# A fused state-space layer and feed-forward block: the last half-operand of each group sum moves from TensorE to VectorE, and the gate moves one scan later

## The reference, cut to what matters

```python
proj = layernorm(x) @ in_proj_w               # 1024 -> 2 x 2048
xc, z = split(proj)                           # channel-major, 2048 channels
xc = silu(conv_b + causal_conv4(xc))
dt, Bm, Cm = rmsnorm of (xc @ x_proj_w)       # 64, 16, 16 columns
dt = softplus(dt @ dt_proj_w + dt_bias)
h[n] = exp(dt * A[n]) * h[n] + dt * Bm[n] * xc   # 16 states per channel, along the rows
ys = sum over n of h[n] * Cm[n]
y  = (ys + D * xc) * silu(z)
x  = x + y @ out_proj_w
x  = x + layernorm(x) @ dequantised(W).T + bias
```

## Time and profile before

| what | us |
| --- | --- |
| median of 3 runs | 4703.04 |
| lowest and highest | 4701.97, 4705.40 |
| the profiled execution | 4697.21 |
| its span in the trace | 4695.4 |
| mean granted TensorE clock | 0.972 of full speed |

### The profile page before, as it was taken

How to read it: one execution, slowest core, us unless ns; L and a number is a source line. 1 busy time by engine, 2 the same in 40 slices (tenths; PEclk the granted TensorE clock), 3 DMA queues, 4 the chain that set the end, 5 groups by cost and what they waited for, 6 DMA issues and landing times.

```text
span 4695.4 us, 80181 instructions
## 1 busy us (share of the span) xinstructions
PE 4448.9 (95%) x26656; PEld 4049.0 (86%) x26656; DVE 4160.0 (89%) x5745; ACT 3542.4 (75%) x8848; POOL 4039.2 (86%) x2942
## 2 busy tenths in 40 slices
PE   7788989999999999999999999999999999999889
PEld 6567879989898998989989898998989889898779
DVE  3898989989899998989989899998989989899981
ACT  3777787877778787777877878787787777778760
POOL 0898989989898998989989898998989899899990
PEclk9889999999999999999999999999999999999999
DMA  7324243353434435343353534334353443434232
GB/s 255 130 79 161 99 159 139 114 186 133 173 129 161 145 138 175 124 178 128 123 188 123 177 137 165 137 128 173 138 180 120 145 165 129 165 127 155 90 115 94
DMA packets 160285, 678.56 MB, mean 145 GB/s; under 512 B 21120, under 2 KB 30080, under 8 KB 110720
## 3 DMA queue, kind: packets, MB, share of 16 engines
q1 hardware_dynamic: 141440, 639.88, 39.0%
q10 hardware_dynamic: 18432, 33.56, 1.9%
HBM read 618.32 MB, written 55.05 MB: 143 GB/s over the span
## 4 chain that ended last, share of the span: by engine, by line
PE 59%; DVE 20%; POOL 7%; issue 6%; ACT 5%; DMA 1%; SPq 0%; DVEq 0%; POOLq 0%; ACTq 0%
PE g L767 13%; PE gx L594 13%; PE ys L574 12%; DVE hb L1342 11%; PE ys L614 9%; PE g L689 4%; POOL dbx L486 4%; DVE hc L1290 4%; DVE gx L1238 2%; POOL half L494 2%; PE ys L604 2%; DVE bst L1218 2%; PE gx L581 2%; ACT hb L1061 1%; PE hb L853 1%
## 5 line engine op out<-in xcount | busy, mean ns | idle before, releaser
L1342 DVE TENSOR_TENSOR_SCAN hb<-hb,dbx 128x512 f32<-128x512 f32 x2048 | 2498.0, 1220 | 108.0 <-ACT hb L1061 84.4
L486 POOL TENSOR_TENSOR dbx<-dtx,bb 128x1024 f32<-128x1024 f32 x1024 | 2421.0, 2364 | 60.1 <-DVE hb L1342 34.9
L1061 ACT ACTIVATE hb<-dt,a_neg 128x256 f32<-128x256 f32 x4096 | 1789.5, 468 | 66.3
L494 POOL TENSOR_TENSOR half<-hc 128x512 f32<-128x512 f32 x1024 | 1303.1, 1273 | 135.4 <-DVE hc L1290 120.4
L1290 DVE TENSOR_TENSOR hc<-hb,cb 128x512 f32<-128x512 f32 x2048 | 1378.9, 673 | 0.0
L574 PE MATMUL ys<-half,ident 128*128 128x256 f32 x4096 | 1073.2, 389 | 133.4 <-POOL half L494 119.2
L574 PEld LDWEIGHTS ys<-half,ident 128*128 128x128 f32 x4096 | 757.2, 194 | 254.3 <-POOL half L494 151.3
L767 PEld LDWEIGHTS g<-wo,ybuf 128*128 128x128 f32 x7680 | 954.0, 198 | 20.2 <-issue 1.3
L767 PE MATMUL g<-wo,ybuf 128*128 128x128 f32 x7680 | 966.7, 281 | 0.6 <-issue 0.6
L614 PE MATMUL ys<-xnT,wz 128*128 128x256 f32 x4096 | 928.8, 380 | 1.6 <-DVE ybuf L1301 1.6
L594 PE MATMUL gx<-xnT,wx 128*128 128x256 f32 x3968 | 904.5, 381 | 4.3 <-DMA wx<-in_win 2.6
(11 more groups left out here) (105 smaller groups left out, 2766.1 us busy)
## 6 DMA issues: line engine op xcount, KB each, us to landing
wz<-in_win SPq DMA_DIRECT2D x128, 1024.0 KB, 4.8
wx<-in_win SPq DMA_DIRECT2D x124, 1024.0 KB, 4.8
wo<-in_wout SPq DMA_DIRECT2D x123, 1024.0 KB, 4.9
wf<-wf_scratch SPq DMA_DIRECT2D x113, 512.0 KB, 3.2
xc_scratch<-xcn ACTq DMA_DIRECT2D x128, 256.0 KB, 2.1
xcs<-xc_scratch SPq DMA_DIRECT2D x128, 256.0 KB, 5.0
bb<-bc_scratch SPq DMA_DIRECT2D x64, 512.0 KB, 7.5
cb<-bc_scratch SPq DMA_DIRECT2D x64, 512.0 KB, 6.7
```

The lines of the kernel that those rows point to most:

```text
L486: nc.gpsimd.tensor_tensor(dbx[:, k % 2, :].rearrange("p (n t) -> p n t", n=NQ), dtx[:, S % 2, a, :].unsqueeze(1).to_broadcast([P, NQ, T]), ...
L494: nc.gpsimd.tensor_tensor(half[:, k % 4, :], hc[:, k % 2, 0:HALF], hc[:, k % 2, HALF:GW], ALU.add).then_inc(halves, 1)
L1061: ins = nc.scalar.activation(h[:, m * T:(m + 1) * T], dt[:, j % 2, a, :], ACT.Exp, scale=a_neg[:, ds((2 * j + a) * N + 2 * v + m, 1)])
L1342: nc.vector.tensor_tensor_scan(h[:], h[:], dbx[:, k % 2, w * UW:(w + 1) * UW], 0.0, ALU.mult, ALU.add).then_inc(scans, 1)
```

## The change

The last group of each half (groups 3 and 7) gets one product on TensorE instead of two. The other operand is added by VectorE onto the PSUM bank (`last_sum`), at the place where the gate stood, and the gate itself comes one scan later. GpSimd waits, before it overwrites the fourth of the four `half` buffers, for the gate that follows the `last_sum` that read it.

```diff
             def group_sum(S, k):
                 pool.wait_ge(hcs, after(UNITS * S + 2 * k + 2))
                 pool.wait_ge(sum_mm, after(8 * S + k - 3))
+                if k % NQ == NQ - 1:
+
+                    pool.wait_ge(y_ready, after(2 * S + k // NQ))
...
                 a, q = divmod(k, NQ)
                 pe.wait_ge(halves, after(8 * SG + k + 1))
-                for i in range(2):
+
+                for i in range(1 if q == NQ - 1 else 2):
                     mm = nc.tensor.matmul(ys[a][:, 0:T], ident[:], half[:, k % 4, i * T:(i + 1) * T],
-                                          start=False, stop=(q == NQ - 1 and i == 1), skip_group_check=True)
+                                          start=False, stop=(q == NQ - 1), skip_group_check=True)
                 mm.then_inc(sum_mm, 1)
...
+            def last_sum(SP, a):
+
+                k = NQ * (a + 1) - 1
+                dve.wait_ge(sum_mm, after(8 * SP + k + 1))
+                dve.wait_ge(halves, after(8 * SP + k + 1))
+                nc.vector.tensor_tensor(ys[a][:, 0:T], ys[a][:, 0:T], half[:, k % 4, T:HALF], ALU.add
+                                        ).then_inc(summed, 1)
+
             def y_gate(SP, a):
 
                 chunk, jp = divmod(SP, PAIRS)
-                dve.wait_ge(sum_mm, after(8 * SP + NQ * (a + 1)))
+                dve.wait_ge(summed, after(2 * SP + a + 1))
...
                     product(1)
+                    late_sum()
+                    scan(3)
                     late_y()
-                    scan(3)
                     product(2)
...
                     product(9)
+                    last_sum(S, 0)
+                    scan(11)
                     y_gate(S, 0)
-                    scan(11)
                     product(10)
...
+            last_sum(LAST - 1, 1)
             y_gate(LAST - 1, 1)
```

More of the change, by code:

```diff
@@ L212, in build_program @@
         a_exp = sem("a_exp")
-        conv, scans, hcs, y_ready = sem("conv"), sem("scans"), sem("hcs"), sem("y_ready")
+        conv, scans, hcs, y_ready, summed = (sem("conv"), sem("scans"), sem("hcs"), sem("y_ready"),
+                                             sem("summed"))
         xp_add, o_add, f_add = sem("xp_add"), sem("o_add"), sem("f_add")
@@ L1352, in late_product, with late_sum @@
                             times_c(S - 1, UNITS - 1)
+                    def late_sum():
+                        if was.scan and not (first and c == 0):
+                            last_sum(S - 1, 1)
                     def late_y():
```

## The result

| us | before | changed |
| --- | --- | --- |
| median | 4702.5 | 4796.8 |
| lowest and highest | 4701.7, 4705.4 | 4792.2, 4797.9 |
| ratio, 95% interval | | 1.0197 (1.018 to 1.0215) |
| profiled execution: span | 4695.4 | 4790.3 |

A forecast was written before the change was run, and what follows sets the result against it. TensorE was taken to set the ordinary interval of 33.20 us. Terms of 79 + 7 - 2 + 6 + 1.5 = + 92 us on 4697.2 gave 4789, with the median 5.8 above it 4795 us; range 4772 to 4838.

The forecast's parts named there:

- The loop: Group 3 on TensorE, VectorE's gates, `x_proj`, back to group 3: 34.17 us against 33.20, 0.97 us longer per ordinary step.
- The price of `last_sum`: Each addition on VectorE, two per step, was taken to cost 0.39 us, with bounds 0.33 and 0.40.
- The stall ahead of `x_proj`: In ordinary steps TensorE idles some 1.6 us for the late gate; VectorE idles some 1.8 us ahead of `last_sum`.
- The other intervals: Those of 34.4, 36.4 and 43.1 us, at each chunk's end, change by + 0.61, + 1.17 and - 0.04 us.
- The clock in the last step: Rival: TensorE's clock falls behind two stalls of about 1.5 us, 12 x 1.75 = + 21 us: 4816; chance 0.25.
- The sum over the chunks: Chunks 2 to 13 add 79 us, chunk 14 7, chunk 1 - 2, chunk 0 6, chunk 15 1.5: + 92 us.
- What was priced at nothing: GpSimd's new waits for gates, and `z_in_proj(1)` on TensorE waiting for the gate of half 0, cost nothing.
- Rival 2: The gate's new place at `x_proj` costs nothing and TensorE's relief counts: - 0.8 us in 67 intervals, 4657 us; chance 0.05.

The follow-up runs named there:

- e5: The kernel before with the late gate alone moved behind scan 3 and no sum moved: 4759.4 us, ratio 1.0131.
- e6: The changed kernel with `x_proj` behind `out_proj(1)` in ordinary steps and behind `out_proj(0)` in steps j = 0 and 7: 4683.3 us, ratio 0.9966.
- e2: The kernel before with both gates moved, behind scan 3 and scan 11, and no sum on VectorE: 4719.0 us, ratio 1.0043.
- e4: The changed kernel with `x_proj` behind `out_proj(1)` on TensorE in ordinary steps, steps j = 0 and 7 as they are: 4701.0 us, ratio 1.0003.
- e1: The changed kernel with both gates back ahead of the scans, right behind the sums on VectorE: 4729.2 us, ratio 1.0066.

## Why the prediction was right, point by point

The forecast was 4795 us and the measurement 4796.8. The mechanism is the one that was forecast; that the number came within 2 us is luck. In chunks 2 to 13 the price of `last_sum` and the intervals that hold it came out 13 us lower, and a fall of the clock that the forecast left to a rival took 13 us more; the two cancel.

- **The loop.** Right, with every part found: in the changed kernel the loop is 0.63 + 18.87 + 0.40 + 0.06 + 14.07 = 34.03 us, and the 0.13 that it is short of the forecast is the price of the two sums. e5 gives the late gate's move (33.20 to 33.81: + 0.61), and the sums give the rest, - 0.43 + 0.34 + 0.33 = + 0.24, against a measured 34.04 - 33.81 = + 0.23. Of + 0.84 us per ordinary step three quarters come from a gate that was moved and one quarter from sums that were added. The prediction had 0.97.
- **The price of `last_sum`** was the mis-sized term: 0.33 to 0.34 us from its start to the next, not 0.39, and a duration of 0.42 us. I had taken it from the convolution, for the write to PSUM that the two have in common; the gate, which has the operation in common, would have been right. The formula of the Trainium skill, "VectorE: DVE Perf Modes", section on the TRN2 errata, gave an estimate of 424 ns, and the trace agrees: the sum's mean on the page of the profile is 424:

```profile
L1304 DVE TENSOR_TENSOR ys<-ys,half 128x256 f32<-128x256 f32 x256 | 108.6, 424 | 243.5 <-PE ys L579 243.0
```

- **The stall ahead of `x_proj`**: 1.6 us predicted, 1.39 measured, and VectorE's wait at the sum 1.8 against 1.88.
- **The other intervals**: + 0.61, + 1.17 and - 0.04 were forecast; + 0.40, + 0.95 and + 0.2 were measured where the clock holds in the last step. Where it falls, the last is - 0.7 (42.3 us against 43.3).
- **The clock in the last step** was a rival with 0.25, and it happened, in every other chunk and for 3.1 us instead of 1.75. In six of twelve chunks that is + 18 us, of which the interval behind gives some 5 back: 13 us, where the forecast had nothing and the rival, in all twelve chunks, 21. I had priced it from a single stall in chunk 1; here the slow stretch was longer. From start to start `x_proj` lost 0.84 us (1.81 against 0.97), and the 16 products of `out_proj(0)` alone 1.67 us of duration (3.62 against 1.95, in the rows of e6's section). In the ordinary steps the stall of 1.39 us left the clock at 1.00, as forecast. The rule quoted from the Trainium skill, "TensorE: Matmul & The Clock Gate", Part 1, that the default state is the throttled one and activity releases it, fits e6, where with work in the second gap the clock stayed at 1.00.
- **The sum over the chunks**: chunks 2 to 13 took 82 us more (79 forecast), chunk 14 took 6 (7), chunks 0 and 1 together 7 (4; chunk 1, forecast at - 2, took + 1), and chunk 15 with the tail nothing (1.5). That is 95 us between the profiled executions, each some 5 us below its median, and 94 between the medians.
- **What was priced at nothing** nearly stayed so: GpSimd's new wait does not appear among the waits, and `z_in_proj(1)` waits for the gate in chunk 0 (1.1 us in most steps, once 3.8), once in chunk 15 (0.4), and 0.1 us in the last step of chunks 2 to 13. I had not seen the second detour, over the feed-forward addition. In the changed kernel it does not bind, for no wait stands ahead of L1277 in the ordinary step; e2 brought it out.

Rival 2, that the relief of TensorE counts, is what e4's ordinary intervals show once 1.8 us of cover are put ahead of `x_proj`: the condition that the prediction gave for it, 1.7 us at that wait, was the right one. Its time, 4657 us, was not reached there: every second ordinary interval stops at 33.05 us, and the last step keeps its stalls.

## What to carry to other kernels

When two engines take turns once per step, their loads do not tell the time of the step; the longest loop through both does. Write down, for each wait from the one to the other, its margin in the profile, and compare what a change adds to the loop, less what it takes out, with that margin: here 1.13 us of a scan and 0.67 of two sums, less 0.43 of a product, against 0.61 us. The scan alone was more than the margin. Then look for work of the waiting engine that can stand in the gap: the same instructions in another order were worth 94 us here.

## What had not been expected of the hardware

Two stalls of TensorE of 1.34 and 1.38 us with 0.66 us of transposes between brought the granted clock down in every other chunk, though a stall of 1.39 us by itself never did in the ordinary steps of chunks 2 to 13, and though both chunks show the same stalls. That the second stall is needed is shown by e6 against e4. The lengths alone do not decide: in e5 the two stalls of the last step are 0.90 and 1.06 us and the clock fell in nine of twelve chunks, in e1 there are three, of 1.11, 1.34 and 0.41 us, and it fell in all twelve. A single stall can do it too: in chunk 0 of the kernel before, one of 1.93 us ended at 230.93 and the clock was at one half from 231.3 to 238.0, while the one of 1.75 us in the earlier trace rows was followed by none. So the length of one stall, by which the prediction called 1.6 us safe, was right for the ordinary steps and no guide for the last one. What decides between two chunks with the same stalls was not found.

And a VectorE instruction that uses the result of the one just ahead, by semaphore, started 0.12 us later than one that doesn't (0.46 against 0.34 us, in all 256 pairs of e1 and of the changed kernel but one). A scan of 1.13 us put between such a pair hides these 0.12 us and costs the rest wherever the pair stands on the longest loop.
